# A convolution with per-sample mixed weights: the weight mix in two units per sample instead of three, and new fixed orders for ScalarE and VectorE

## What is computed

```python
pooled = jnp.mean(x, axis=(2, 3))                 # x is already group-normalised here
att = jax.nn.sigmoid(pooled @ att_w.T + att_b)    # N x 4
agg_w = jnp.einsum('nk,kocij->nocij', att, weight)
out = jax.vmap(conv_one)(x, agg_w)                # 3x3, padding 1, 256 -> 256
...
x = x + _L0_conv_ref(_gn(x), L0_conv_weight, L0_conv_att_w, L0_conv_att_b)
```

## Time and profile before

| what | value |
|---|---|
| median of 3 runs | 1317.84 us (1317.57 to 1319.83) |
| profiled execution, first to last instruction | 1316.9 us |
| around that span, up to the median | 0.9 us |
| TensorE, VectorE, ScalarE busy | 97%, 92%, 69% of the span |
| TensorE's mean granted clock | 0.996 of full speed |

### The profile page before, as it was taken

One profiled execution on the slowest core, in us unless ns is written; L12 is line 12 of the kernel. 1 busy time (PEld: TensorE's weight loads), 2 busy tenths in 40 slices (PEclk: granted clock), 3 DMA queues, 4 the chain that ended last, 5 costly groups with the idle time before them and its releaser, 6 DMA issues.

```text
span 1316.9 us, 23092 instructions
## 1 busy us (share of the span) xinstructions
PE 1278.7 (97%) x8656; PEld 725.8 (55%) x8656; DVE 1207.7 (92%) x2119; ACT 913.4 (69%) x1442; POOL 56.8 (4%) x72
## 2 busy tenths in 40 slices
PE   2899999999999999999999999999999999999998
PEld 0355555555555555555555555555555555555555
DVE  7999999999999999999899998999999899998983
ACT  4966877867767676776767767676867766777531
POOL 0000000000000000000000000000000000000000
PEclk9899999999999999999999999999999999999999
DMA  9215645457553545535255552545535254552434
GB/s 378 109 65 147 183 108 142 143 142 211 130 132 91 150 120 148 148 69 152 77 148 144 132 147 62 133 116 148 147 77 151 80 151 132 148 147 56 103 93 143
DMA packets 30763, 174.59 MB, mean 133 GB/s; under 512 B 3520, under 2 KB 3776, under 8 KB 28352
## 3 DMA queue, kind: packets, MB, share of 16 engines
q1 hardware_dynamic: 20432, 113.94, 23.4%
q0 software_dynamic: 8928, 49.78, 22.5%
q10 hardware_dynamic: 1296, 9.44, 1.8%
HBM read 112.33 MB, written 51.38 MB: 124 GB/s over the span
## 4 chain that ended last, share of the span: by engine, by line
PE 83%; DVE 9%; ACT 3%; DMA 2%; issue 2%; SPq 0%; ACTq 0%; DVEq 0%; POOLq 0%
PE pM L472 76%; PE pG L437 6%; DVE Vs L648 1%; DMA W<-w_dram 1%; DMA X<-x_dram 1%; DVE W L897 1%; DVE T L591 1%; DVE E L616 1%; DVE E L630 1%; ACT Us L1110 1%; DVE X L755 1%; DVE X L743 1%; ACT unused L1088 1%; DVE T L624 0%; ACT Us L1033 0%
## 5 line engine op out<-in xcount | busy, mean ns | idle before, releaser
L472 PE MATMUL pM<-Vs,Us 128*128 128x385 f16 (+1 forms) x6912 | 1158.9, 330 | 1.6 <-DVE Us L643 1.3
L472 PEld LDWEIGHTS pM<-Vs,Us 128*128 128x128 f16 x6912 | 672.6, 98 | 486.4 <-issue 18.3
L1018 ACT CAST Vs<-E 128x784 f16<-128x784 f32 x192 | 159.9, 840 | 119.9 <-DVE E L616 61.2
L591 DVE SCALAR_TENSOR_TENSOR T<-X 128x392 f32<-128x392 f32 x384 | 193.4, 559 | 12.0 <-ACT X L1076 10.0
L648 DVE TENSOR_TENSOR Vs<-E,Vs 128x784 f16<-128x784 f32 x192 | 182.1, 968 | 0.7 <-ACT Vs L1018 0.7
L1033 ACT ACTIVATE Us<-E 128x768 f16<-128x768 f32 x120 | 96.4, 836 | 50.1 <-DVE E L630 50.1
L616 DVE SCALAR_TENSOR_TENSOR E<-T 128x784 f32<-128x784 f32 x128 | 119.1, 972 | 2.2
L437 PE MATMUL pG<-W,D 128*32 128x512 f16 (+1 forms) x1628 | 112.2, 418 | 9.3 <-ACT G L1070 4.8
L630 DVE SCALAR_TENSOR_TENSOR E<-G,T 128x768 f32<-128x768 f32 x128 | 117.0, 955 | 2.2
L1096 ACT ACTIVATE unused<-X,small 128x784 bf16<-128x784 f32 x120 | 113.8, 948 | 4.2 <-ACT small L1092 0.3
L643 DVE SCALAR_TENSOR_TENSOR Us<-E,Us 128x768 f16<-128x768 f32 x120 | 111.7, 951 | 0.2
(11 more groups left out here) (81 smaller groups left out, 595.4 us busy)
## 6 DMA issues: line engine op xcount, KB each, us to landing
X<-x_dram SPq DMA_DIRECT2D x66, 784.0 KB, 5.4
out_dram<-X SPq DMA_DIRECT2D x64, 784.0 KB, 3.8
X<-x_dram POOLq DMA_DIRECT2D x62, 784.0 KB, 8.1
W<-w_dram SPq DMA_DIRECT2D x9, 1024.0 KB, 20.3
G<-W ACTq DMA_DIRECT2D x9, 1024.0 KB, 4.8
attw<-attw_dram SPq DMA_DIRECT2D x1, 128.0 KB, 8.3
small<-attb_dram SPq DMA_DIRECT2D x1, 0.5 KB, 10.3
```

Source lines behind the costliest of these rows:

```text
L472: mm = pe.matmul(tile_rows(bank(k, o))[:, :, first:last], Us[:, j, a, c, o, kx, :], v_in(j, b, c, kx), start=(at < 2 and i == 0), stop=(i ...
L591: ins = dve.scalar_tensor_tensor(out=dst[c], in0=a[c], scalar=scale, in1=d[c], op0=ALU.mult, op1=ALU.add)
L1018: act.copy(v_out(j, 0), e_buf(n, ("V", chunk, j))).then_inc(v_hi, 1)
```

## The change

TensorE's order within samples 1 to 14: the nine mix tiles come in two units, tiles 0 to 4 between the groups of slot 8 and those of slot 9, and tiles 5 to 8 between the two groups of slot 9. Within slot 0 the two groups change places. Sample 0 keeps three units. The wait for `attention` moves into tile 0.

ScalarE and VectorE keep the same operations in a new order, and the tables of orders get a row each for the first, the second and the later samples. The loops of SyncE and GpSimd are written out. The diff, cut to its core:

```diff
+TAKES_ACT_LATER = [
+    (0, 1), (0, 0), (1, 0), (1, 1), (2, 0), (2, 1), (3, 0), (3, 1), (6, 0), (6, 1), (7, 0), (7, 1), (8, 1),
+    (8, 0), (9, 0), (9, 1)
+]
...
             for chunk in range(CH):
@@ -422,6 +439,8 @@
             def mix_tile(n, m):
                 if not is_first(n) or m >= MIX_BANKS:
                     pe.wait_ge(taps_taken, n * TAKES + m - MIX_BANKS + 1)
+                if m == 0:
+                    pe.wait_ge(att_ready, n + 1)
                 if is_first(n):
...
-            def mix(n, u):
-                if u == 0:
-                    pe.wait_ge(att_ready, n + 1)
-                for m in range(MIX_BANKS * u, MIX_BANKS * (u + 1)):
-                    mix_tile(n, m)
-
             def group(n, k, o):
                 chunk, at = k // NC, k % NC
                 j = ORDER[at]
-                if o == 0:
-                    pe.wait_ge(v_lo, count(V_LO, n, [(chunk, j)]))
-                    if chunk == 0:
-                        pe.wait_ge(u_lo, count(U_LO, n, [(c, j) for c in range(CT)]))
+                pe.wait_ge(v_lo, count(V_LO, n, [(chunk, j)]))
+                if chunk == 0:
+                    pe.wait_ge(u_lo, count(U_LO, n, [(c, j) for c in range(CT)]))
                 if at < 2:
 
                     if chunk:
@@ -476,8 +488,8 @@
                 mm.then_inc(group_done, 1)
 
...
             def epoch(n, more):
+                group(n, 0, 1)
                 group(n, 0, 0)
-                group(n, 0, 1)
                 group(n, 1, 0)
                 group(n, 1, 1)
...
                     logits_mm(n + 1)
                 group(n, 7, 0)
                 group(n, 7, 1)
-                if more:
-                    mix(n + 1, 0)
                 group(n, 8, 0)
                 group(n, 8, 1)
                 if more:
-                    mix(n + 1, 1)
+                    mix_tile(n + 1, 0)
+                    mix_tile(n + 1, 1)
+                    mix_tile(n + 1, 2)
+                    mix_tile(n + 1, 3)
+                    mix_tile(n + 1, 4)
                 group(n, 9, 0)
+                if more:
+                    mix_tile(n + 1, 5)
+                    mix_tile(n + 1, 6)
+                    mix_tile(n + 1, 7)
+                    mix_tile(n + 1, 8)
                 group(n, 9, 1)
-                if more:
-                    mix(n + 1, 2)
                 group(n, 10, 0)
                 group(n, 10, 1)
                 group(n, 11, 0)
...
                 u_low(n, 1, 0)
                 u_low(n, 0, 0)
                 u_low(n, 0, 4)
+                v_pair(n, b, 1, 1)
                 u_low(n, 1, 5)
-                v_pair(n, b, 1, 1)
                 v_low(n, 0, 5)
                 v_low(n, 0, 0)
+                u_low(n, 0, 5)
+                v_single(n, b, 1, 5)
                 take_other(n, 2, 0)
-                v_single(n, b, 1, 5)
-                u_low(n, 0, 5)
                 v_low(n, 1, 1)
+                take_other(n, 2, 1)
                 take_other(n, 3, 0)
-                take_other(n, 2, 1)
+                v_pair(n, b, 1, 3)
+                take_other(n, 3, 1)
                 v_low(n, 1, 2)
                 take_edge(n, b, 4, 0)
-                v_pair(n, b, 1, 3)
-                take_other(n, 3, 1)
+                take_edge(n, b, 4, 1)
                 if more:
                     channel_stats(n + 1)
                     group_shift(n + 1)
-                take_edge(n, b, 4, 1)
-                if more:
                     group_variance(n + 1)
                 v_single(n, b, 1, 0)
+                take_edge(n, b, 5, 0)
                 if more:
                     norm_scale(n + 1)
                 v_low(n, 1, 3)
-                take_edge(n, b, 5, 0)
+                add_rows(n, b, 3, 1)
                 v_low(n, 1, 5)
                 take_edge(n, b, 5, 1)
-                v_low(n, 1, 0)
                 add_rows(n, b, 3, 0)
+                v_low(n, 1, 4)
                 if len(split_in(n)) > 0:
                     w_low(n, 0)
-                v_low(n, 1, 4)
+                v_low(n, 1, 0)
                 if more:
                     attention(n + 1)
+                    v_pair(n + 1, 1 - b, 0, 1)
                 if len(split_in(n)) > 1:
                     w_low(n, 1)
-                add_rows(n, b, 3, 1)
-                if more:
-                    v_pair(n + 1, 1 - b, 0, 1)
+                if more:
                     v_pair(n + 1, 1 - b, 0, 3)
+                    v_low(n + 1, 0, 2)
                     v_low(n + 1, 0, 1)
                     v_low(n + 1, 0, 3)
-                    v_low(n + 1, 0, 2)
                     u_pair(n + 1, 0, 1)
                 take_other(n, 8, 0)
                 take_other(n, 9, 0)
@@ -835,25 +859,26 @@
                 if more:
                     u_low(n + 1, 0, 1)
                     u_low(n + 1, 0, 2)
+                    v_low(n + 1, 0, 4)
                 take_other(n, 9, 1)
                 if more:
-                    v_low(n + 1, 0, 4)
                     u_pair(n + 1, 1, 1)
                     u_pair(n + 1, 1, 3)
                     u_low(n + 1, 1, 1)
                     take_edge(n, b, 10, 0)
                     take_edge(n, b, 10, 1)
                     take_edge(n, b, 11, 0)
+                    u_low(n + 1, 1, 3)
+                    u_low(n + 1, 1, 2)
                     add_rows(n, b, 9, 1)
-                    u_low(n + 1, 1, 2)
                     u_pair(n + 1, 0, 3)
-                    u_low(n + 1, 1, 3)
                     u_low(n + 1, 0, 3)
                     take_edge(n, b, 11, 1)
                     v_single(n + 1, 1 - b, 0, 0)
-                    u_low(n + 1, 1, 4)
                 if not more:
                     last_takes(b)
+                if more:
+                    u_low(n + 1, 1, 4)
 
...
             def epoch(n, b, more):
-                u_high(n, 0, 0)
+                u_high(n, 1, 2)
                 u_high(n, 1, 3)
-                u_high(n, 1, 2)
+                if more:
+                    sums(n + 1, 1 - b, 0, 0)
                 u_high(n, 1, 0)
-                if more:
-                    sums(n + 1, 1 - b, 0, 0)
+                u_high(n, 0, 3)
                 u_high(n, 1, 4)
-                u_high(n, 0, 3)
                 u_high(n, 0, 5)
                 take_first(n, 0, 1)
+                u_high(n, 0, 0)
                 u_high(n, 1, 5)
                 take_first(n, 0, 0)
                 take_first(n, 1, 0)
                 v_high(n, 0, 0)
+                v_high(n, 0, 5)
                 u_high(n, 0, 4)
                 if more:
                     sums(n + 1, 1 - b, 0, 1)
-                v_high(n, 0, 5)
                 take_first(n, 1, 1)
                 v_high(n, 1, 2)
                 take_pair(n, b, 2, 0)
                 v_high(n, 1, 1)
                 take_pair(n, b, 2, 1)
-                take_pair(n, b, 3, 0)
-                if more:
-                    sums(n + 1, 1 - b, 1, 0)
                 if split_in(n):
                     w_aside_too(n)
+                take_pair(n, b, 3, 0)
+                if more:
+                    sums(n + 1, 1 - b, 1, 0)
                 take_pair(n, b, 3, 1)
                 if more:
                     sums(n + 1, 1 - b, 1, 1)
                 v_high(n, 1, 3)
+                v_high(n, 1, 4)
                 if len(split_in(n)) > 0:
                     w_high(n, 0)
                 if more:
                     root(n + 1)
                 v_high(n, 1, 5)
-                v_high(n, 1, 0)
                 if len(split_in(n)) > 1:
                     w_high(n, 1)
-                v_high(n, 1, 4)
-                if more:
+                v_high(n, 1, 0)
+                if more:
+                    norm(n + 1, 1 - b, 1, 1)
                     norm(n + 1, 1 - b, 1, 0)
+                    norm(n + 1, 1 - b, 0, 0)
                     exponential(n + 1)
-                    norm(n + 1, 1 - b, 0, 0)
-                    norm(n + 1, 1 - b, 1, 1)
+                take_first(n, 6, 0)
+                if more:
                     norm(n + 1, 1 - b, 0, 1)
-                take_first(n, 6, 0)
                 take_first(n, 6, 1)
                 if more:
                     v_high(n + 1, 0, 1)
-                    take_taps(n + 1, 0)
-                    take_taps(n + 1, 1)
-                    take_taps(n + 1, 2)
                 take_first(n, 7, 0)
                 take_first(n, 7, 1)
                 if more:
+                    v_high(n + 1, 0, 2)
+                    take_taps(n + 1, 0)
+                take_pair(n, b, 8, 1)
+                if more:
+                    take_taps(n + 1, 1)
                     v_high(n + 1, 0, 3)
-                take_pair(n, b, 8, 0)
-                if more:
-                    v_high(n + 1, 0, 2)
+                    take_taps(n + 1, 2)
                     take_taps(n + 1, 3)
                     take_taps(n + 1, 4)
-                take_pair(n, b, 8, 1)
+                    take_taps(n + 1, 5)
```

(65 more changed lines are left out.)

129 lines of the change are left out of this document (69 added, 60 removed), and 14 rows, old and new, of tables (E_FIRST, E_LATER, E_NEXT).

## The result

The changed kernel takes 1312.45 us (median of 5 executions, 1311.98 to 1314.47), against 1317.84 us before (5 executions, 1317.56 to 1319.83). The ratio is 0.9958 with a 95% interval from 0.9947 to 0.9969: 5.4 us faster, which is more than the 2.6 us that this measurement can tell from no change. The forecast was 1313.2 us.

The account below looks back on a forecast made before the run. TensorE, busy for 1278.7 of 1316.9 us, was taken as the bound. 1316.9 - 2.8 (units) - 2.2 (waits) + 0.4 (thin margin) gave a span of 1312.3 us, 0.9 more as median: 1313.2 us, range 1312.0 to 1316.8.

Parts of the forecast that it names:

- Term 1: TensorE's mix: one unit less in each of samples 1 to 14, at 0.20 us each, takes 2.8 us off.
- third rival: Little changes but the waits: a longer unit pays the 0.20 us elsewhere; 1.8 us off, 1316.0 us; chance 0.08.
- Term 2: Samples 1 to 3: the first unit starts 5.98 us later, so TensorE's waits go; 2.2 us off.
- Terms 3 and 4: SyncE and GpSimd loops written out, and slot 0's two groups swapped on TensorE: 0 us each.
- The thin margin: First unit: tile 4 needs tile 1's copy, ready 0.08 us early; 0.04 us charged in 11 samples, 0.4 us.
- second rival: Copies fall behind: `take_pair` between ScalarE's copies makes tile 4 wait; 1.8 us more, 1315.0 us; chance 0.13.
- VectorE's lag: VectorE 2.0 us later at `take_other` (8, 0); margins 0.4 at group (1, 0), 0.3 at (4, 0); no wait charged.
- The sum: Whole kernel: span 1316.9 - 2.8 - 2.2 + 0.4 = 1312.3 us, plus 0.9 from span to median, 1313.2 us.

Follow-up runs that it names:

- experiment 2: Changed kernel with mix tile 8 moved behind group (9, 1), making a third unit of one tile; 1316.27 us, ratio 0.9982, 78.61 us per sample.
- experiment 3: Changed kernel with all nine mix tiles in one unit between slots 8 and 9, ScalarE and VectorE reordered to suit; 1311.61 us, ratio 0.9946.
- experiment 4: Kernel before with only the loops of SyncE and GpSimd written out; 1317.57 us, ratio 0.9993.
- experiment 10: Changed kernel unaltered, run again beside others on the same chip; median 1314.3 us, ratio 0.9965.
- experiment 7: Changed kernel with ScalarE's `v_high(0, 3)` ahead of the copy of tile 1 instead of behind it; 1326.75 us in one execution.
- experiment 5: Changed kernel with one extra VectorE memset of unused PSUM columns per sample after `take_other` (8, 0); 1316.63 us in one execution.
- experiment 8: One-unit kernel of experiment 3 with VectorE's `u_low(0, 1)` moved between `take_other` (8, 0) and (9, 0); 1310.38 us, ratio 0.9936.
- experiment 1: Kernel before with only TensorE's two new units, ScalarE and VectorE keeping their old orders; 1324.2 us, ratio 1.0046.
- experiment 11: Changed kernel with eight filler matmuls where TensorE waits for sample 0's `u_low`; 1312.81 us, ratio 0.9957.
- 9: Kernel of experiment 8 with eight filler matmuls where TensorE waits for sample 0's `u_low`; 1309.74 us, ratio 0.9931.

## Why the prediction was right

The time of each step here is moved by -2.77 us against the prediction, since sample 8 starts at 729.30 in place of 732.07.

**Term 1, the unit.** 0.22 us and not 0.20: the difference per sample, and again experiment 2's. 14 x 0.22 = 3.1 where I had 2.8. It is a cost per unit and not per tile, since in experiment 3 nine tiles and the step back still take 5.94. The Trainium skill, TensorEngine Tiling (Array Packing), section "Key Properties", has a drain at each change of tiling mode, and all four unit counts here (three, two, one, three again: 78.61, 78.39, 78.17 and 78.61 per sample) agree with that. That a drain is what fills the 0.22 us, no run shows. The third rival, that a longer unit pays the 0.20 elsewhere, fell.

**Term 2, the waits.** Samples 1 to 3 are 2.90 shorter, 3 x 0.22 of it from the units, so 2.24 from the waits; forecast 2.2. Some of that belonged to the one execution it was read from: in experiment 4 TensorE doesn't wait for `attention` in sample 3, which takes 80.47 there and not 80.74. Between experiments 4 and 10 the waits make 2.64 - 0.66 = 2.0.

**Terms 3 and 4.** Experiment 4 confirms 0 for the loops within the span, and shows 0.35 us outside of it that I had put at nothing. For the swap in slot 0 there is no experiment of its own; the distances of samples 5 to 13 leave nothing for it.

**The thin margin.** I had charged 0.4 us for it and it cost nothing: TensorE has no wait in the first unit. Besides the first term and the loops, that is the one that was mis-sized. ScalarE's rows follow the predicted times within 0.06 us:

```profile
741.82 0.85 ACT L1042 CAST Vs<-E 128x784 f16<-128x784 f32 x1 [1.79 <-PE pM L484]
742.66 0.60 ACT L1094 ACTIVATE G<-pG 128x512 f32<-128x512 f32 x1
743.15 0.58 ACT L1078 ACTIVATE X<-pM,small 128x392 f32<-128x392 f32 x1
743.62 0.60 ACT L1094 ACTIVATE G<-pG 128x512 f32<-128x512 f32 x1
744.10 0.85 ACT L1042 CAST Vs<-E 128x784 f16<-128x784 f32 x1
```

The copy of tile 1 was to start at t0 + 1.87, 743.59, and starts at 743.62; it ends at 744.22, TensorE could go on 0.06 later, and tile 4 is due at 741.72 + 2.60 = 744.32. The margin of 0.08 us was 0.04, it held, and experiment 7 shows what lies behind it. By the Trainium skill, TensorEngine Tiling (Array Packing), section "PSUM Bottleneck", the copies may become what limits. As long as two copies are only `take_pair` apart the trace does not agree, and with one conversion more between them it does: the deciding thing is what stands between the copies, as the second rival had it.

**VectorE's lag.** VectorE of the kernel after in order of time: ahead of `take_other` (8, 0) and (9, 0), and at the two places of small margin:

```profile
750.80 0.62 DVE L761 SCALAR_TENSOR_TENSOR TA<-pM,small,TA 128x392 f32<-128x392 f32 x1 [1.52 <-ACT X L1078]
751.34 0.61 DVE L761 SCALAR_TENSOR_TENSOR TB<-pM,small,TB 128x392 f32<-128x392 f32 x1
...
770.37 0.96 DVE L666 SCALAR_TENSOR_TENSOR Us<-E,Us 128x768 f16<-128x768 f32 x1
...
788.71 0.62 DVE L761 SCALAR_TENSOR_TENSOR TA<-pM,small,TA 128x392 f32<-128x392 f32 x1
```

`take_other` (8, 0) was forecast for 753.55 - 2.77 = 750.78 after an idle time of about 1.6, and is at 750.80 after 1.52. `u_low(0, 3)` ends at 771.33 (forecast 774.1 - 2.77 = 771.3), `take_other` (2, 0) starts at 788.71 (forecast 791.5 - 2.77 = 788.7). Group (4, 0) starts 13 groups after the second unit, 750.87 + 13 x 2.99 = 789.74, and its operand is there at 789.33: the margin of 0.4 less a latency, which experiment 5 measured as 0.27.

**The sum.** Against the median the forecast was 1317.84 - 4.6. With 0.22 a unit and without the 0.4 it is 3.1 + 2.2 = 5.3 us off; with the waits at 2.0, sample 0's loss of 0.1 and the 0.35 of the loops it is again 5.3. The medians differ by 5.4. That this fits to 0.1 us is luck, since the first input alone moves an execution by up to 1.9; the terms rest on the distances and not on it. That the profiled span, 1312.6, lies so near the 1312.3 of the text is luck too. That execution lost about 1.7 us to the clock, and started 0.7 earlier: TensorE waited 22.1 us for the input of its first `logits_mm`, in place of 22.8 in the kernel before, whose list of TensorE's waits has these two rows:

```profile
PE pS L418 <- DVE small L709: 22.8, 1, 22.8
PE pM L472 <- DVE Us L643: 1.3, 1, 1.3
```

The 0.7 us are the first loads' own spread: experiment 4 starts at 22.1 with the old orders, experiment 7 at 23.0 with the new ones. The second row is one that the prediction left out when it said that TensorE waits for 0.6 and 1.3 us only once the first group runs: a further 1.3 us are a wait for `u_low` in sample 0. The change doesn't touch it and the sum doesn't need it, but it is the place of the clock's drop, which I had not foreseen.

The 0.9 us that I carried from span to median is no property of the kernel either. Times of the kernel before lie about 2.15 us above their span, so its profiled execution took some 1319.05 us and was itself 1.2 above its median; the changed kernel's lie 1.8 above (1314.39 and 1312.6). Since I used the high span and the low offset together, that slip cancelled.

## What to carry to other kernels

When two kinds of matmul share TensorE, count how often it steps between them: here each trip costs 0.22 us whatever its length, and nine tiles in one trip (78.17 per sample in experiment 8) beat two trips (78.39) and three (78.61). The same move alone made the kernel slower, because a unit that goes away also takes away the cover of whatever ran beside it; so before merging, list for each group which result it waits for and when that is done, and move those first. And fill an engine's wait for one result with an operation that it owes anyway (0.11 us a sample in experiment 8), for on an engine that is 92% busy a pause can come back later as lateness.

## What the runs showed of the hardware that I had not expected

The changed kernel's executions come in two kinds, five of ten between 1311.98 and 1312.45 with a mean granted clock of 0.997, and five from 1314.3 to 1315.57 with 0.996. The profiled one is of the second kind. So do those of the kernel before: of 30 beside experiments 1 to 4 and 8 to 11, 11 have 0.996 (1319.26 to 1320.56) and 19 have 0.997 (1317.15 to 1319.32), so the change didn't bring this. TensorE of it in the head, then the engines' busy times, and the granted clock (PEclk), from 60 to 70 us in the kernel after and, under it, in experiment 11:

```profile
60.05 10.14 PE L484 MATMUL pM<-Vs,Us 128*128 128x392 f16 x50 [2.11 <-DVE Us L666]
...
60.00:70.00 10.00, 9.96 (x50) 5.46 (x51) 9.93 (x15) 9.43 (x18) 0.00 (x0) 0.83 0.01 2
```

```profile
58.24 1.47 PE L533 MATMUL pS<-Vs 128*128 128x384 f16 x8
60.06 10.13 PE L484 MATMUL pM<-Vs,Us 128*128 128x392 f16 x60 [0.36 <-DVE Us L667]
...
60.00:70.00 10.00, 9.94 (x60) 5.90 (x61) 9.93 (x15) 9.84 (x20) 0.00 (x0) 1.00 0.01 2
```

TensorE stands 2.11 us waiting for `u_low`, and then its clock is at the lower of its two levels, 1.2 GHz, for 3.4 us: 50 matmuls where 60 fit. Nine groups take 88.63 - 60.05 = 28.58 us, where they took 87.71 - 60.80 = 26.91 before, 1.7 more. In the kernel before's profile the wait was 1.26 us and the clock stayed at 2.4 GHz (1.00 in this stretch). The wait's length is no matter of the kernel: experiment 10, the changed kernel again, has 1.47, and experiment 1, with the old orders, 2.10. In the six profiles with waits of 1.26 to 1.76 us the clock stays. But a wait of 2.1 us doesn't always lower it: experiments 1, 3 and 8 have it and no drop, experiment 5 has the drop. With the eight fillers the wait is 0.36 us in experiment 11 and below what is listed in 9, and none of their ten executions has a mean below 0.997. That the drop is what makes all the higher executions is likely from their clock and from what the filler does to them, but only the profiled ones were seen, and what decides between drop and no drop after the same wait stays open.
